# A feed-forward stage's weight preparation, cut into three pieces between matmul groups, with its low-rank terms stacked into single fp32r passes

## The reference, cut to what matters

```python
def _matmul_lora(x, w, a, b, scale=1.0):
    out = jnp.einsum('bsd,hd->bsh', x, w)
    out = out + jnp.einsum('bsr,hr->bsh', jnp.einsum('bsd,rd->bsr', x, a), b) * scale
    return out
gate = _matmul_lora(x, gate_w, gate_a, gate_b)       # 512 -> 1376, rank 16
up = _matmul_lora(x, up_w, up_a, up_b)               # 512 -> 1376, rank 16
hidden = jax.nn.silu(gate) * up
out = _matmul_lora(hidden, down_w, down_a, down_b)   # 1376 -> 512, rank 16
```

## Time and profile before

| | us |
|---|---|
| median of 3 runs | 1949.35 |
| lowest and highest | 1948.03, 1955.16 |
| the profiled execution's own time | 1956.68 |
| its span in the profile | 1954.9 |
| mean granted TensorE clock | 0.949 |

### The profile page before, as it was taken

How to read it: one execution, slowest core, us unless ns; L and a number is a source line. 1 busy time by engine, 2 the same in 40 slices (tenths; PEclk the granted TensorE clock), 3 DMA queues, 4 the chain that set the end, 5 groups by cost and what they waited for, 6 DMA issues and landing times. The chain is left out here.

```text
span 1954.9 us, 25185 instructions
## 1 busy us (share of the span) xinstructions
PE 1798.7 (92%) x9130; PEld 1303.3 (67%) x9130; DVE 1144.5 (59%) x2249; ACT 810.2 (41%) x1780; POOL 867.3 (44%) x768
## 2 busy tenths in 40 slices
PE   5799999999999999999997999988859999999778
PEld 3567777677776777767774677767645555555457
DVE  6856656566575665656566222224787666664465
ACT  3445455454454545545453111100315555656221
POOL 1686786868868688686760000000252222220200
PEclk9899999999999999999998688889879999999889
DMA  5110111111010110101003111000400000000021
GB/s 179 33 33 28 33 31 30 32 29 33 21 39 19 42 33 17 38 17 33 28 1 100 50 34 50 13 0 27 145 1 1 1 1 1 1 2 1 28 42 44
DMA packets 75732, 63.09 MB, mean 32 GB/s; under 512 B 23838, under 2 KB 53886, under 8 KB 75610
## 3 DMA queue, kind: packets, MB, share of 16 engines
q1 hardware_dynamic: 75610, 61.49, 10.6%
HBM read 59.37 MB, written 2.10 MB: 31 GB/s over the span
## 5 line engine op out<-in xcount | busy, mean ns | idle before, releaser
L844 ACT ACTIVATE a_probs<-psum,a_neg_max 128x128 f32<-128x128 f32 (+7 forms) x256 | 190.3, 743 | 265.4 <-DVE a_neg_max L768 265.0
L768 DVE CUSTOM_DVE_ANT_0 psum<-psum,a_keys_allowed 128x128 f32<-128x128 f32 (+7 forms) x256 | 195.4, 764 | 134.4 <-PE psum L77 134.1
L698 PE MATMUL psum<-a_probsT,a_v 128*128 128x512 f32 (+3 forms) x768 | 258.4, 486 | 0.2 <-ACT a_probsT L855 0.2
L1587 DVE TENSOR_REDUCE a_neg_max<-psum 128x1 f32<-128x512 f32 (+3 forms) x384 | 194.8, 552 | 102.0 <-PE psum L1507 67.4
L698 PEld LDWEIGHTS psum<-a_probsT,a_v 128*128 128x128 f32 x768 | 144.6, 190 | 117.3 <-issue 91.8
L1650 ACT ACTIVATE a_probsT<-psum 128x512 f32<-128x512 f32 (+3 forms) x384 | 173.5, 494 | 93.6 <-PE psum L1488 69.1
L780 DVE SCALAR_TENSOR_TENSOR x<-psum,a_row_inv,x 128x512 f32<-128x512 f32 x256 | 191.2, 749 | 16.9 <-PE psum L77 10.3
L855 ACT COPY a_probsT<-psum 128x512 f32<-128x512 f32 (+3 forms) x384 | 171.1, 484 | 9.7 <-PE psum L685 9.6
L685 PE MATMUL psum<-ident,a_probs 128*128 128x128 f32 x1152 | 171.7, 274 | 0.5 <-ACT a_probsT L855 0.4
L785 DVE TENSOR_TENSOR a_ctxT_lo<-psum,a_ctxT_hi 128x512 fp32r<-128x512 f32 x64 | 44.3, 692 | 215.9 <-ACT a_ctxT_hi L861 215.9
L75 PE MATMUL psum<-a_kT_hi,a_qT_lo 128*128 128x512 f32 (+3 forms) x384 | 150.6, 392 | 21.6 <-POOL a_qT_lo L567 21.6
(11 more groups left out here) (286 smaller groups left out, 4137.9 us busy)
## 6 DMA issues: line engine op xcount, KB each, us to landing
a_raw_q<-in_L_attn_qw_q SPq DMA_DIRECT2D x32, 256.0 KB, 4.1
a_raw_o<-in_L_attn_qw_o SPq DMA_DIRECT2D x32, 256.0 KB, 2.7
a_raw_scale_o<-in_L_attn_scales_o SPq DMA_DIRECT2D x32, 256.0 KB, 3.6
mod1b_w<-in_L_wmod SPq DMA_DIRECT2D x4, 1024.0 KB, 12.6
mod0a_w<-in_L_wmod SPq DMA_DIRECT2D x3, 1024.0 KB, 10.2
mod0b_w<-in_L_wmod SPq DMA_DIRECT2D x3, 1024.0 KB, 8.7
f_raw<-in_L_ffn_down_w SPq DMA_DIRECT2D x10, 256.0 KB, 3.2
f_raw<-in_L_ffn_gate_w SPq DMA_DIRECT2D x10, 256.0 KB, 3.4
```

What stands on the lines that cost most here:

```text
L698: last = nc.tensor.matmul(bank(use)[:, first:HALF], v[:, g % 2, j, :], probsT[b][:, j, first:HALF], start=(j == 0), stop=(j == keys - 1))
L768: nc.vector.tensor_tensor_reduce(out=scores, in0=scores, in1=keys_allowed[:, S - (i + 1) * P:S], scale=-1.0, scalar=-MASKED, op0=ALU.add, ...
L844: nc.scalar.activation(probs[:, u % 3, 0:(i + 1) * P], score[u % 2][:, 0:(i + 1) * P], ACT.Exp, bias=neg_max[:, h % 2, i:i + 1], scale=-1. ...
L1587: nc.vector.reduce_max(neg_max[:, c, i, h:h + 1], y_bank[n % SLOTS][:, 0:keys], AX.X, negate=True).then_inc(maxed.sem, 1)
```

## The change

- PE's work on tile f+1 is cut into three pieces which stand between the four groups of project(f), each group 12 matmuls (one matrix, one half): the `b` factors and the down weight after the first group, gate after the second, up after the third. `turn_b`, `turn_down` and `turn_in` are the pieces; only tile 0 is prepared ahead of the loop.
- `projected` is now signalled for gate and up apart. Silu waits for gate's two groups; gate's first group waits for the silu of the tile before and no longer for its multiply; up's first group waits for the multiply.
- The low-rank factors are stacked along the contraction: rows 0 to 15, 32 to 47 and 64 to 79 hold the high part of b, again the high part, and the low part, against the high part, the low part and again the high part of a. One fp32r matmul of 80 rows takes the place of an fp32 matmul of 16 rows (`STACK` = 80).
- All low-rank factors are loaded at once in the layer norm's block, 14 transfers behind a wait for POOL's first three clears, and ahead of tile 0's weights and the gate's modulation weights. POOL has a new program there, `stack_low`: it clears, rounds and stacks the factors. `load_tile` has three transfers left.
- `raw` moves to the other side of SBUF, where the low part of `act_t` later takes its place.

The diff, cut to its core:

```diff
-        raw_b = sb("raw_b", [P, 2, 2, RANK0])
-        low_a = sb("low_a", [RANK0, 2, D])
+        b_stack, down_b_stack = sb("b_stack", [P, NF, 2, STACK]), sb("down_b_stack", [P, KT, STACK])
+        low_a, down_a = sb("low_a", [STACK, 2, D], F32R), sb("down_a", [STACK, HID], F32R)
...
         def loads(sp):
             for n in (3, 4):
                 modulation.load(sp, n)
-            sp.dma_start(down_b[:, :, :], w["down_b"].rearrange("(k p) r -> p k r", p=P)).then_inc(low_in, 16)
-            sp.dma_start(low_a[:, 0, :], w["gate_a"][:, :]).then_inc(low_in, 16)
-            sp.dma_start(low_a[:, 1, :], w["up_a"][:, :]).then_inc(low_in, 16)
-            load_tile(sp, 0, 0)
+            sp.wait_ge(low_step, RAW_ZEROED)
+            for m, name in enumerate(("gate", "up")):
+                sp.dma_start(raw_b[:, 0:LAST, m, :],
+                             w[name + "_b"][0:FULL_ROWS, :].rearrange("(f p) r -> p f r", p=P)).then_inc(low_in, 16)
+                sp.dma_start(raw_b[0:HID_LAST, LAST, m, :], w[name + "_b"][FULL_ROWS:HID, :]).then_inc(low_in, 16)
+            sp.dma_start(raw_down_b[:, :, :], w["down_b"].rearrange("(k p) r -> p k r", p=P)).then_inc(low_in, 16)
+            for rows in (HI, ALSO_HI, LO):
+                sp.dma_start(raw_a[rows, 0, :], w["gate_a"][:, :]).then_inc(low_in, 16)
+                sp.dma_start(raw_a[rows, 1, :], w["up_a"][:, :]).then_inc(low_in, 16)
+                sp.dma_start(raw_down_a[rows, :], w["down_a"][:, :]).then_inc(low_in, 16)
+            load_tile(sp, 0)
             modulation.load(sp, 5)
-            load_tile(sp, 1, 1)
+            load_tile(sp, 1)
+        def stack_low(pool):
+            for buffer in (raw_b[:, LAST, :, :], raw_a[:, :, :], raw_down_a[:, :]):
+                pool.memset(buffer, 0.0).then_inc(low_step, 1)
...
+            pool.wait_ge(low_in, 16 * LOW_LOADS)
...
+                for columns in (HI, ALSO_HI):
+                    pool.tensor_tensor(pick(stack, columns).bitcast(F32R), source, zeros_like, ALU.add).then_inc(low_step, 1)
+            for source, out in ((flat_raw_a, flat_a), (raw_down_a[:, :], down_a[:, :])):
+                pool.tensor_tensor(out, source, zeros(source), ALU.add).then_inc(low_step, 1)
...
-            layernorm_phase(nc, mem, 1, loads, modulation)
-        down_bT = sb("down_bT", [RANK0, D])
-        low_bT = sb("low_bT", [RANK0, 2, 2, P])
+            layernorm_phase(nc, mem, 1, loads, modulation, {"gpsimd": stack_low, "scalar": lambda act: None})
+        down_bT = sb("down_bT", [STACK, D], F32R)
+        low_bT = sb("low_bT", [STACK, 2, 2, P], F32R)
...
-            def project(g, s, f):
-                r = rows_of(f)
-                pe.wait_ge(*w_split.now(g, (s, 1)))
-                pe.wait_ge(*(hidden_done.now(g, 0) if s else hidden_done.last(g, 1)))
-                for m in range(2):
-                    for b in range(NHALF):
-                        for k in kts:
-                            last = split_products(nc.tensor, out_pair[m][:r, half(b)], [part[:, s, m, k, 0:r] for part in wT],
-                                                  [part[:, k, half(b)] for part in mem.hT], k == 0, k == KT - 1)
-                last.then_inc(projected.sem, 1)
-
-            run_turns(pe, prepare, project)
-            project(TURNS, 0, LAST)
+            def project(f, m, b):
+                r, s = rows_of(f), f % 2
+                if b == 0:
+                    pe.wait_ge(*w_split.now(f, m))
+                    pe.wait_ge(*(hidden_done.last(f, "up") if m else silu_done.last(f, "gate")))
+                for k in kts:
+                    last = split_products(nc.tensor, out_pair[m][:r, half(b)], [part[:, s, m, k, 0:r] for part in wT],
+                                          [part[:, k, half(b)] for part in mem.hT], k == 0, k == KT - 1)
+                if b == NHALF - 1:
+                    last.then_inc(projected.sem, 1)
+
+            turn_b(0)
+            turn_down(0)
+            turn_in(0, 0)
+            turn_in(0, 1)
+            for f in tiles:
+                project(f, 0, 0)
+                if f < LAST:
+                    turn_b(f + 1)
+                    turn_down(f + 1)
+                project(f, 0, 1)
+                if f < LAST:
+                    turn_in(f + 1, 0)
+                project(f, 1, 0)
+                if f < LAST:
+                    turn_in(f + 1, 1)
+                project(f, 1, 1)
```

More of the change, by code:

```diff
@@ L994, in _, with turn_b @@
                 counter.open(pe)
[L995 removed]
+            pe.wait_ge(low_step, STACKED)
             for k in kts:
[L997 removed]
+                last = nc.tensor.transpose(small_bank[:STACK, k * P:(k + 1) * P], down_b_stack[:, k, :], mem.ident[:, :])
             last.then_inc(down_bT_turned, 1)
             pe.wait_ge(down_bT_out, 1)
[L1001 removed]
+            def turn_b(f):
@@ new lines, in turn_in @@
+            def turn_in(f, m):
+                r, s = rows_of(f), f % 2
+                pe.wait_ge(*w_split.last(f, m))
+                if m == 0:
+                    pe.wait_ge(*bT_out.now(f, "b"))
+                for k in kts:
+                    nc.tensor.matmul(wT_bank[m][:, k * P:k * P + r], raw[:r, s, m, k * P:(k + 1) * P],
+                                     mem.ident[:r, :r], is_transpose=True, start=(k == 0), stop=False)
+                for k in kts:
+                    last = nc.tensor.matmul(wT_bank[m][:, k * P:k * P + r], low_a[:, m, k * P:(k + 1) * P],
+                                            low_bT[:, s, m, 0:r], start=False, stop=(k == KT - 1))
+                last.then_inc(wT_turned.sem, 1)
@@ L1066, in prepare @@
                                ).then_inc(bT_out.sem, 1)
-                for m in range(2):
-                    act.wait_ge(*wT_turned.now(g, (s, m)))
-                    act.wait_ge(*projected.last(g, s))
-                    nc.scalar.copy(wT[0][:, s, m, :, 0:r],
-                                   wT_bank[m].rearrange("p (k n) -> p k n", k=KT)[:, :, 0:r]).then_inc(w_hi.sem, 1)
-            def silu(g, s, f):
-                r = rows_of(f)
-                act.wait_ge(*projected.now(g, s))
-                nc.scalar.activation(hidden[:r, bass.ds(f, 1), :], out_pair[0][:r, :], ACT.Silu).then_inc(silu_done.sem, 1)
@@ L1078, in _, with take_in, silu @@
-            run_turns(act, prepare, silu)
-            silu(TURNS, 0, LAST)
+            def take_in(f, m):
+                r = rows_of(f)
+                act.wait_ge(*wT_turned.now(f, m))
+                if f >= 2:
+                    act.wait_ge(*projected.now(f - 2, m))
+                nc.scalar.copy(wT[0][:, f % 2, m, :, 0:r],
+                               wT_bank[m].rearrange("p (k n) -> p k n", k=KT)[:, :, 0:r]).then_inc(w_hi.sem, 1)
+            def silu(f):
+                r = rows_of(f)
+                act.wait_ge(*projected.now(f, 0))
+                nc.scalar.activation(hidden[:r, f, :], out_pair[0][:r, :], ACT.Silu).then_inc(silu_done.sem, 1)
@@ L1081, in _ @@
+            take_b(0)
+            take_in(0, 0)
+            take_in(0, 1)
+            for f in tiles:
+                if f < LAST:
+                    take_b(f + 1)
+                silu(f)
+                if f < LAST:
+                    take_in(f + 1, 0)
+                    take_in(f + 1, 1)
         @block.vector
@@ new lines, in take_in, with multiply @@
+            def take_in(f, m):
+                r = rows_of(f)
+                dve.wait_ge(*w_hi.now(f, m))
+                nc.vector.tensor_tensor(wT[1][:, f % 2, m, :, 0:r],
+                                        wT_bank[m].rearrange("p (k n) -> p k n", k=KT)[:, :, 0:r],
+                                        wT[0][:, f % 2, m, :, 0:r].bitcast(F32), ALU.subtract
+                                        ).then_inc(w_split.sem, 1)
+            def multiply(f):
+                r = rows_of(f)
+                dve.wait_ge(*silu_done.now(f, "gate"))
+                dve.wait_ge(*projected.now(f, 1))
+                nc.vector.tensor_tensor(hidden[:r, f, :], out_pair[1][:r, :], hidden[:r, f, :], ALU.mult
```

177 lines of the change are left out of this document (84 added, 93 removed).

## The result

Four runs of the changed kernel have a median of 1894.31 us (1891.85 to 1896.51); four runs of the kernel before on the same chip have 1952.26 (1948.03 to 1957.62). The ratio is 0.9691, with a 95% interval of 0.9668 to 0.9714: about 58 us faster. Three later comparisons of the same two kernels gave 0.9712, 0.971 and 0.9715.

A forecast was written before the change was run, and what follows sets the result against it. PE's work and clock were taken as the bound. Loop -53.0 us (passes 21.6, clock 23.0, low-level prepare 5.9, wait 2.5), its end -1.0, layernorm block +7: -47 from 1949.35, so 1902 us, range 1888 to 1918.

The forecast's parts named there:

- Fewer passes: Loop's prepare work: fp32r passes take L1017 from 1.05 to 0.23 us and L1026 from 1.09 to 0.52; 21.6 us gained.
- the one that kept the transposes at 0.75 and 0.58: Prepare work per tile: transposes unchanged at 0.75 us (b and down) and 0.58 each (gate, up), within 3.18.
- 80 rows in place of 16 cost nothing: Stacked matmuls in the loop: more rows add no time, as project's matmuls have 128; size 0.
- The prologue and the slow start: Loop's start: one prepare step at the low clock, 3.18 x 1.84 = 5.9 us, plus 2.5 for one slow clock rise.
- The clock: Feed-forward loop: cutting the 5.14 us prepare step into short pieces keeps the clock at 1.00, gaining 23.0 us.
- The rival in which the clock falls as now: Loop: the clock still falls once a tile, pieces or not; ten falls of 2.3 us return, 1925 us; 8%.
- Waits in the loop: PE in the loop: other engines keep up, all waits cost nothing, and the 2.46 us before the last tile goes.
- The layer norm's block: Block before the feed-forward: POOL's stacking beside DVE's subtractions and casts lengthens it by 7 us, ends +1 and +14.
- the sign "near 1084": Layer norm's block: POOL's last row expected near 1084 on the profile's time axis, if the forecast was right.
- The end of the loop: After the last project matmul: the last silu no longer stands behind it, 1.0 us gained.
- The stacked matmul gaining nothing: Loop's L1026: weight load or format makes it as slow as two fp32 passes; 1914 us, 1923 with L1017; 6%.
- the double block of +14: Layer norm's block costs double the +7 taken, small transfers being the least certain price; 1909 us; 14%.

The follow-up runs named there:

- stacking issued twice: Stacked factors in the old one-piece order, each prepare step's transposes and stacked matmuls issued twice, against the changed kernel: 1926.27 us, loop 182.8.
- stacking as plain fp32: Old one-piece order, stacked 80-row factors multiplied as plain fp32 in two passes, against the changed kernel: 1918.42 us, loop 178.1.
- stacking only: The changed kernel's stacked factors, but prepare and project each in one piece in the old order: 1907.24 us, ratio 0.9785, loop 162.6.
- split stacking: Changed kernel with ACT rounding, POOL's clears after DVE's first statistics, a's low parts and later tiles' stacking in the feed-forward block: 1891.86 us, block 30.8.

## Why the prediction was right, and where its steps were off

- **The time.** 1902 us was forecast and 1894 measured, inside the range; the faster case held. In its own terms, the touched part gained 52.8 us and not 47: 61.0 in the loop, less 7.6 in the block, 0.2 between the block and the loop, and 0.4 behind the loop. The medians lie 58 us apart; the 5 us beyond the touched part are not explained by it. In the profiled pair, 10.4 us lie in later code that is the same in both, at different clocks.
- **Fewer passes.** L1017 became 0.32 us (0.23 taken), and L1026 0.48 (0.52 taken). The step that was mis-sized is the one that kept the transposes at 0.75 and 0.58. They were read as transposes' time, but 0.2 us of each belonged to the plain fp32 passes of 16 rows behind them: four take 0.35 ahead of an fp32r matmul, 0.44 ahead of plain passes of 80 rows, 0.53 ahead of 16. So the pieces of a tile take 2.55 us (0.57 for the `b` factors and down's transposes, 0.32, and twice 0.35 + 0.48), not 3.18. With what they add to the project matmuls behind them a tile takes 13.79, 2.66 more than its project matmuls alone, which is 5.2 us less than forecast over ten tiles. The remark that 80 rows in place of 16 cost nothing was too careful: they gain (4.23 us a step, not 5.14, with the passes unchanged).
- **The prologue and the slow start.** 4.95 us, not 5.9, for the same reason, and 1.4 for the slow start, not 2.5 (155.4 less the prologue, ten tiles of 13.79 and one project step of 11.1). With the 5.2 this is 7.2 of the 8.0 us by which the loop beat its forecast; the rest is project's pace, just below 0.233.
- **The clock.** 23 us were forecast from it, and the loop agrees: 1.00 from 4 us into tile 0. But the argument gave the length of today's step as the reason, and that is not what the runs show. A stacked step of 5.07 us in one piece keeps the clock, and stacking alone cures it, as the order alone does. Nor does each of the falls before come with a step: the one before the last tile comes at the end of PE's wait of 2.46 us. The rival in which the clock falls as now could have come true only if both cures had failed. The Trainium skill's rule (page "TensorE: Matmul & The Clock Gate", section "Part 4: PE-mode transpose"), by which the full clock does not come with transposes, is not borne out: twice as many transposes, in one piece, ran at 1.00.
- **Waits in the loop.** None, as forecast; the 2.46 us is gone. That uncut steps would have cost nine more waits, of 0.57, once they were short, was not foreseen.
- **The layer norm's block.** +7.6, where +7 was taken and the Trainium skill's rule ("SBUF — State Buffer", section "Who interferes with whom") gave +9. Its mechanism is shown: without POOL's chain the block is 30.6, and clear of overlap, with all the work done, 30.5. POOL began 15.5 us into the block (15.1 forecast) and worked for 14.5 (15.4). It ended at 1077.45, 30.1 us into the block (30.5 by the working), so the sign "near 1084" did not come. The block ends with DVE alone, 7 us later. The estimate named only the subtractions and casts. The scaling (0.17 to 1.28) was missed, and so were DVE's copies beside POOL's clears (0.63 to 3.95 us), which cost the block nothing. A memset has no input, so for the copies the part of the rule on two inputs would not do; the same section of the Trainium skill has the pair taken by a copy in a two-port mode too. No run here shows in which mode these copies ran.
- **The end of the loop.** 1.0 us was forecast there, for the silu no longer behind the last matmul. PE's wait before the down matmuls did fall from 2.95 to 1.97 us. But the stretch from the loop's end to the next layer norm took 67.0 us, against 66.7 before: the down matmuls, unchanged, stood 0.233 us apart in place of 0.227 towards its end. Why is not known.
- **The rivals.** The stacked matmul gaining nothing, and the double block of +14, were both excluded by rows: 0.32 and 0.48 us, and 38.0.

## What to carry to other kernels

When two parts of a change can each cure the same loss, their gains don't add: run each alone before saying which one did it (28.8 and 53.9 us alone were 61.0 together). A distance between starts belongs to both instructions at its ends, so a term held fixed in a forecast should be one whose neighbours stay the same. Work for an idle POOL is not free where DVE is on the path: here it was moved to where DVE waits for PE, roundings went to ACT, and the clear that others wait for was put ahead of it in POOL's queue, and the 7.6 us of the block went down to 0.1. A stretched instruction is not yet a cost: DVE's copies took five times as long (3.33 us for 0.63), and the block ended at most 0.2 us later. And a row that shows a full clock speaks only for its own window; the falls of two runs here lie just behind theirs.

## What the runs showed of the hardware

- A plain fp32 matmul of 16 rows was slower than the same of 80 rows: eight passes of 128 columns 1.08 against 0.90 us, two of 512 columns 1.05 against 0.97, and the transposes ahead of it stretched too. The Trainium skill (page "TensorE: Matmul & The Clock Gate", section "LDWEIGHTS (loading the stationary operand)") has a weight load cost the same at any number of rows; the trace agrees in its load rows, 0.96 us for eight loads with 16 rows and 0.97 with 80. The difference is in when the first of them starts: with 80 rows 0.11 us ahead of its matmul (1129.42, 1129.53), with 16 rows together with it (1134.72).
- The granted clock fell from 2.4 to 1.2 GHz in each tile only where an uncut step had plain fp32 passes of 16 rows. PE did not wait in these steps; its only wait in that loop is the 2.46 us before the last tile. The clock also fell where that wait ended, in the kernel before, in stacking issued twice and in stacking as plain fp32, but not in stacking only. Behind the loop of the changed kernel it fell after a wait of 1.97 us (0.50 at 1246 to 1249).
- DVE's 128x512 cast took 3.30 us in place of 0.42 beside one POOL subtraction of 3.42, and its four copies 3.95 in place of 0.63 beside POOL's memsets. Its statistics (L252) took 2.46 with the memsets beside them for 1.7 us (split stacking), as before.
- Loads of 3264 pieces of 64 bytes cost at most 0.2 us in the block (30.6 against 30.4), though they held SP's queue: two issues took 2.14 and 3.23 us.
